# Two Mamba scans: convolution taps and gate of the first four channel tiles taken in the even slot, the time steps' chain alone in the odd one

## The reference

```python
zxbcdt = x @ in_proj_w.T                       # z 1024, xBC 1152, dt 16
dt = softplus(dt + dt_bias)
xBC = silu(conv(xBC, conv_w) + conv_b)         # causal, 4 taps, each channel by itself
xs, B, C = split(xBC)                          # 1024, 64, 64
dA = exp(dt * -exp(A_log))
h = h * dA_t + (dt_t * x_t) B_t                # scan over the 1024 tokens, 16 heads
y_t = h C_t
y = (ys + D * xs) * silu(z)
y = y * rsqrt(mean(y * y) + 1e-5) * rms_w
return y @ out_proj_w.T
```

## Time and profile before

| what | us |
|---|---|
| time, median of 3 runs | 4943.44 (4933.94 to 4956.82) |
| the profiled execution | 4941.54 |
| its span | 4939.4 |
| PE busy in the span | 4366.1 |
| DVE busy | 3085.8 |
| ACT busy | 1487.3 |
| POOL busy | 1046.1 |

### The profile page before, as it was taken

One profiled execution on the slowest core, in us unless ns is written; L12 is line 12 of the kernel. 1 busy time (PEld: TensorE's weight loads), 2 busy tenths in 40 slices (PEclk: granted clock), 3 DMA queues, 4 the chain that ended last, 5 costly groups with the idle time before them and its releaser, 6 DMA issues. The chain is left out here.

```text
span 4939.4 us, 62871 instructions
## 1 busy us (share of the span) xinstructions
PE 4366.1 (88%) x23000; PEld 2976.2 (60%) x23000; DVE 3085.8 (62%) x6572; ACT 1487.3 (30%) x2991; POOL 1046.1 (21%) x631
## 2 busy tenths in 40 slices
PE   7999999987989898986789779779888969999999
PEld 5667677755666666663544444454364447777777
DVE  5888888854888888886543344245234356666664
ACT  3433343323333333331134124214213411111111
POOL 1333333330444444444000000100100000000000
PEclk8999999998999999998877988889888879999999
DMA  2011111002111111111321321232132130000000
GB/s 97 35 38 36 37 38 38 33 15 87 36 46 40 40 36 46 40 37 53 129 78 33 119 82 48 96 101 60 57 116 68 39 105 26 31 30 26 30 26 22
DMA packets 146922, 265.55 MB, mean 54 GB/s; under 512 B 27188, under 2 KB 33336, under 8 KB 146616
## 3 DMA queue, kind: packets, MB, share of 16 engines
q1 hardware_dynamic: 144568, 261.27, 16.0%
q10 hardware_dynamic: 2048, 0.27, 0.0%
HBM read 164.58 MB, written 88.08 MB: 51 GB/s over the span
## 5 line engine op out<-in xcount | busy, mean ns | idle before, releaser
L1721 DVE TENSOR_REDUCE xa_mx<-xa_s 128x1 f32<-128x1024 f32 (+7 forms) x512 | 371.4, 746 | 343.7 <-PE xa_s L1795 336.1
L1623 ACT ACTIVATE xa_src<-xa_gen 128x512 f32<-128x512 f32 (+3 forms) x768 | 357.4, 491 | 547.4 <-PE xa_gen L1815 396.5
L1812 PE MATMUL xa_gen<-xa_qa,xa_ka 98*128 98x512 f32 (+3 forms) x768 | 351.6, 487 | 84.0 <-ACT xa_src L1623 52.4
L72 PE MATMUL ff_wb<-ff_w_hi,ff_st_hi 128*128 128x512 f32 x768 | 322.8, 420 | 17.1 <-DVE ff_parts L2308 11.1
L1572 POOL TENSOR_TENSOR xa_kq<-xa_kq 128x512 f32<-128x512 f32 x32 | 40.8, 1274 | 1374.8 <-DVE xa_kq L1727 1374.8
L1794 PE MATMUL xa_s<-xa_ka,xa_qa 97*128 97x512 f32 (+3 forms) x768 | 255.1, 398 | 78.5 <-DVE xa_mx L1721 55.8
L1812 PEld LDWEIGHTS xa_gen<-xa_qa,xa_ka 98*128 98x128 f32 x768 | 167.9, 222 | 251.0 <-issue 121.8
L73 PE MATMUL ff_wb<-ff_w_hi,ff_st_lo 128*128 128x512 f32 x768 | 310.2, 404 | 0.0
L74 PE MATMUL ff_wb<-ff_w_lo,ff_st_hi 128*128 128x512 f32 x768 | 309.4, 403 | 0.0
L1203 PE MATMUL mb_ib<-mb_wc,mb_yT 128*128 128x512 f32 x512 | 268.0, 672 | 1.8 <-DVE mb_y L974 1.0
L1203 PE MATMUL mf_ib<-mf_wc,mf_yT 128*128 128x512 f32 x512 | 249.6, 633 | 1.8 <-DVE mf_y L974 1.0
(11 more groups left out here) (513 smaller groups left out, 11395.6 us busy)
## 6 DMA issues: line engine op xcount, KB each, us to landing
xa_qa<-xa_q_dram SPq DMA_DIRECT2D x384, 64.0 KB, 2.0
xa_ka<-xa_k_dram SPq DMA_DIRECT2D x384, 64.0 KB, 2.0
xa_q_dram<-xa_kq SPq DMA_DIRECT2D x32, 512.0 KB, 2.8
xa_k_dram<-xa_kq SPq DMA_DIRECT2D x32, 512.0 KB, 2.8
mf_xg<-in_x_dram SPq DMA_DIRECT2D x16, 512.0 KB, 5.2
turned_dram<-mf_xt_hi SPq DMA_DIRECT2D x16, 512.0 KB, 2.6
turned_dram<-mf_xt_lo SPq DMA_DIRECT2D x16, 512.0 KB, 4.0
part_dram<-mf_hb SPq DMA_DIRECT2D x32, 256.0 KB, 2.0
```

What stands on the lines that cost most here:

```text
L72: nc.tensor.matmul(out, w_hi, x_hi, start=first, stop=False)
L1623: a_.activation(pe_x[:, s % 2, hh, 0:w], gen["p2", g, s, hh][:, 0:w], ACT.Exp, scale=XSCALE)\
L1721: v_.tensor_reduce(mx[:, g % 2, i, hh:hh + 1], s1[g, hh, i][:, 0:(i + 1) * P], AX.X, ALU.max)\
L1812: last = mm(ps[:, 0:n], ka[sl][0:ROW_MAX + 1, j * P:(j + 1) * P], qa[sl][0:ROW_MAX + 1, a:a + n], start=True, stop=not diagonal)
```

## The change

The yields of `order()` move. `silu` of part 0 goes from the odd to the even slot, behind the taps. The step `taps` takes a part as second number: part 0 (the 12 taps of tiles 0 to 3, one after the other) comes before `back` 3 and 4, part 1 (prefix sums and the 15 taps of the back tiles) where `taps` stood. `front` on DVE keeps the chain alone. On PE, the output projection's bank is opened behind the first pair of exponents instead of ahead of it. The number of operations stays the same.

```diff
                 if n % 2 == 0 and 0 <= n // 2 + 1 < NGF:
+                    yield "taps", (n // 2 + 1, 0)
                     for i in range(3, MP):
                         yield "back", (n // 2 + 1, i)
-                    yield "taps", n // 2 + 1
+                    yield "taps", (n // 2 + 1, 1)
...
-                if n % 2 and 0 <= (n + 3) // 2 < NGF:
-                    yield "silu", ((n + 3) // 2, 0)
+                if n % 2 == 0 and 0 <= n // 2 + 1 < NGF:
+                    yield "silu", (n // 2 + 1, 0)
                 if -1 <= n < N:
                     yield "mixed", n
...
                 step(v_.reciprocal(wb[:], wa[:]))
-                conv = taps(g, 0)
-                next(conv)
                 step.after()
                 step(v_.tensor_tensor(wd[:], ea[:], wb[:], ALU.mult))
-                next(conv)
                 step.after()
...
                 step(v_.scalar_tensor_tensor(dt[:, r], wb[:], 2.0, wt[:], ALU.mult, ALU.add))
-                finish(conv)
                 step.after()
...
-            def taps_back(g):
+            def convolved(g, p):
                 r = g % 2
+                if p == 0:
+                    finish(taps(g, 0))
+                    return
                 wait(dve, cs_full, g)
...
                     wait(pe, yT_ready, 2 * n + 1)
-                    ps = ib.open(pe, ("o", n))
                 for k in range(KI):
                     if c < N and k % 4 == 0:
                         decays(c, k // 4)
+                    if n >= 0 and k == 0:
+                        ps = ib.open(pe, ("o", n))
                     if n >= 0:
                         last = mm(ps[:], yT[:, k, :], wc[:, k, :], start=k == 0, stop=k == KI - 1)
```

More of the change, by code:

```diff
@@ L1034, in output @@
                 v_.tensor_scalar(h, h, hmv[:, 0:1], hr[:, 0:1], ALU.subtract, ALU.mult).then_inc(n_ready.sem, 1)
-            run({"split": split, "consts": consts, "norm": norm, "xT": turn_in, "halo": halo, "steps": steps, "front": front, "taps": taps_back, "silu": silu, "mixed": mixed,
+            run({"split": split, "consts": consts, "norm": norm, "xT": turn_in, "halo": halo, "steps": steps, "front": front, "taps": convolved, "silu": silu, "mixed": mixed,
                  "carry": carry, "total": total,
```

## The result

The changed kernel takes 5057.74 us (median of 4 runs, 5051.98 to 5071.86) against 4946.74 for the kernel before in the same comparison (4 runs). The ratio is 1.023, 95% interval 1.0197 to 1.0263: slower by 2.3%, 111 us. The profiled execution took 5056.0 us, its span is 5053.2.

A forecast was written before the change was run, and what follows sets the result against it. Forward was taken as nearly PE's own work, backward as losing time in odd slots where DVE is late. Forward 14 x (4.5 - 0.8 + 1.0) = +66, backward 14 x 2.1 = +29: 5038 us, range 4965 to 5090.

The forecast's parts named there:

- Forward, even slot, +4.5: Forward even slot: taps 5.0, gate 1.15 and a hold 0.9, less waits 1.43 and 0.98 and slack 0.1: +4.5 us.
- Forward, odd slot, -0.8: Forward odd slot: removing taps and gate gains only 0.8 us, since the state then waits for z.
- Clock forward, +1.0 a pair: Forward PE clock: new idle time in even slots costs +1.0 us net a pair, bounds 0 and 2.2.
- Backward, taps 12.0 us: Backward even slot: twelve taps take turns with five POOL operations and need about 12.0 us, not 5.0.
- The bound of 5.0: Backward even slot: the twelve taps' lower limit in us, if the taps win over POOL each time.
- The bound of 12.7: Backward even slot: the twelve taps' upper limit in us, in full turn-taking with POOL.
- Backward, odd slot: Backward odd slot: state_ready at 21.7 to 22.4 us where it is 28.2, slot length 31 to 33 us.
- The output bank, 0: Bank opened behind the first exponents: 0 in a normal slot, as the second exponent still needs the state.
- Backward, +2.1 a pair: Backward pair: +7.3 even, -6.2 odd, +1.0 waiting for z, net +2.1 us, between -4 and +3.9.
- the gain of 6.2: Backward odd slot: DVE's part shrinks by 6.2 us without the taps, waited tanh and gate.
- the two with the taps winning over POOL: Taps keep POOL out backward: 4945 us, no change (chance 0.09), or 4892 us, faster (chance 0.08).
- The heavier one (5074): Holds stretch fully and the forward clock loses 2.2: forward 5.4, backward 3.9 us a pair, 5074 us; chance 0.20.

The follow-up runs named there:

- Experiment 1: The kernel before with only the output bank opened behind the first exponents: 4947.61 us, ratio 1.0004.
- 2: The kernel before with the whole change in the forward scan only, the bank moved in both scans: 5014.25 us, ratio 1.0144.
- 3: The kernel before with the whole change in the backward scan only, the bank moved in both scans: 4990.87 us, ratio 1.0096.
- 7: The changed kernel with the forward scan's norm moved from the even to the odd slot, behind the steps' chain: 4975.68 us, ratio 1.0062.
- 6: The changed kernel with two POOL operations on the finished row (L637, L639) left out in the backward scan: 5017.39 us, ratio 1.0136 to the kernel before.
- 5: The kernel before with two POOL operations on the finished row (L637, L639) left out in the backward scan: 4887.96 us, ratio 0.9879.
- Experiment 4: The kernel before with only the gate (tanh and L870 of tiles 0 to 3) moved to the even slot: 4900.06 us, ratio 0.9906.

## Why the prediction was right

The forecast was 5038, range 4965 to 5090; the time is 5057.74. Going through its own steps:

- **Forward, even slot, +4.5.** The state comes 26.9 us after the start instead of 22.4 (541.71 + 0.68 against 515.5): 4.5. Its parts are in the timeline above: taps 5.09 (5.0), gate 1.15, one tap held by L609, 0.78 (0.9).
- **Forward, odd slot, -0.8.** The length of the slot shown is 31.1 for 31.9, and the state stands at 21.9 for 22.6.
- **Clock forward, +1.0 a pair: nearly right, for the ordinary pairs.** The 13 pairs grew by 69.6 us (902.0 for 832.4), 5.4 each; taking off 4.5 - 0.8 leaves 1.7. In the ten ordinary pairs it is 1.2: even slots lose to the half clock that follows the new wait (38.1 us, 6.4 more, where the state is 4.5 later), and odd slots that had lost some clock before get it back (32.6 to 31.1 on average). The rest is not clock: the three even slots that follow the end of a sequence took 39.1 to 41.8 us for 30.5. There PE no longer waits in the odd slot before (29.1 us long), so DVE is 7.6 us behind it at the start instead of 2.4, and the prefix sums begin at 17.4. That lag I had not foreseen.
- **Backward, taps 12.0 us.** They took 11.34. The bound of 5.0 would have needed the taps to go first each time; they took turns. The bound of 12.7 adds POOL's work to the taps' in full, but one tap passes ahead of each POOL operation.
- **Backward, odd slot.** The state is at 21.9, in the 21.7 to 22.4 given, and the length 31.1, in the 31 to 33 given.
- **The output bank, 0.** Experiment 1 shows nothing beyond its 12 us.
- **Backward, +2.1 a pair: too small.** It is 42.3 / 13 = 3.3. Two terms are off. First, the gain of 6.2 was read from an odd slot of 40.2 us, one of the longest; the thirteen have a mean of 38.5. The pair that was read (72.5 us) became one of 74.9, so +2.4. Even this closeness is partly luck, since two misses cancel: from the odd slot's state to the even one's DVE needed 40.7 us for 34.4, +6.3 where 7.3 was forecast, and from there to the odd slot's state 34.2 for 38.1, -3.9 where -5.2 was forecast. Second, this -3.9 is where the sentence "DVE carries the pair there, so PE's slower clock is not added" failed. After the wait of 10 us in each even slot PE runs at the half clock: from the state to the next slot it needs 12.3 us at a mean clock of 0.74, against 9.3 at 1.00 in the odd slot. So PE comes late to the next odd slot, and there z is PE's to give. In the steady scan DVE waits for z's tanh for 36.3 us now, all of it in odd slots, 2.8 us each where 1.0 was allowed:

```profile
DVE mb_zs L962 <- ACT mb_zs L756: 6.9, 9, 1.0
...
DVE mb_zs L958 <- ACT mb_zs L757: 36.3, 13, 3.8
```

Of the rivals, the two with the taps winning over POOL fell with the 11.34 us. The heavier one (5074) had the right place: the time lies between it and the forecast, and its forward figure of 5.4 us a pair is the measured one. Its backward 3.9 is not worked out in the prediction, and its condition there, holds that stretch fully, did not come about: the taps took less than 12.0.

The cause in one line: 5 us of DVE work went from slots in which it held PE up by 0.8 us forward (about 6 backward, POOL's holds and the gate included) to slots in which all of it holds PE up, less a wait of 1.43 forward, and less 5.9 backward, which POOL's turns ate. Experiments 2, 3 and 7 show the forward half. Backward, 3 shows the size, 6 that the taps take turns with POOL, and every run with all twelve taps late that the odd slot stops near 31 us; but 5 and 6 together show that the change would lose there with less POOL work as well, and no run has POOL out of the taps' way altogether, so how the loss divides between the turns and z is read from the timelines, not shown by an experiment. Experiment 4 shows that the gate, moved alone, is a gain; with POOL's three operations moved too, the kernel takes 4877 us, less than both.

## What to carry to other kernels

An engine's idle time before a wait is room only if nothing else uses what the moved work needs. Look at the other engines' rows over the same stretch: here DVE's 5.9 us of idle lay exactly under 7.9 us of POOL. Ask too when the idle engine enters the slot once the slot before is shorter: here 7.0 us after PE instead of 4.2. And ask in which slot the engine's lateness reaches the end. Taking work out of a slot gains only down to the next producer (here z, after 0.8 us forward), while adding it costs in full where the slack is 0.1. When a change bundles several moves, try each alone: here one of them was worth -44 us and hid behind one that cost far more.

## What the runs showed of the hardware

- DVE operations with two inputs in SBUF and POOL operations held each other up in both directions here, and a stream of back-to-back taps did not keep POOL out: they took turns, one tap to one POOL operation. Twelve taps took 5.09 us with POOL idle, 8.27 beside two POOL operations on the inputs, 9.41 beside these two and one on the finished row, and 11.34 beside five. POOL's L638 took 1.46 us instead of 1.28.
- An operation with one input was held too. L901, a TENSOR_SCALAR of 128x32, took 1.05 us backward, issued under POOL's L639 (1604.03 to 1605.31), and 0.18 forward:

```profile
467.80 0.18 DVE L901 TENSOR_SCALAR mf_wa<-mf_ea 128x32 f32<-128x32 f32 x1 [0.29 <-ACT mf_ea L717]
...
1604.30 1.05 DVE L901 TENSOR_SCALAR mb_wa<-mb_ea 128x32 f32<-128x32 f32 x1 [0.30 <-ACT mb_ea L717]
```

- The same short waits did not always cost clock. Forward, before the change, PE idles for 0.9 + 0.7 us in every ordinary odd slot. Six of the ten took 31.9 us, four took 33.5 to 33.6; the granted clock was 1.00 in one of the first kind (from 458.7) and 0.95 in one of the second (from 522.2). With the gate moved only 0.8 us of idle remained, all ten took 31.1 us, and the clock was 1.00 over the window. With 3.3 + 0.7 us of waits in the even slots it was 0.95.
